# Loads of x in slots 10 to 16, the first convolution of the next image at the head of slot 10, and a gather without its tie to TensorE, in a kernel of grouped convolution and deformable bottleneck

## The reference

```python
x = x + _L0_conv_ref(_gn(x), W, b)           # 3x3, 8 groups; its result reshaped (B,G,gout,L)->(B,G,L,gout)->(B,512,32,32)
x = x + _L1_conv_ref(_gn(x), ...)            # the deformable bottleneck
# _L1_conv_ref:
out = relu(bn1(conv1x1(x, conv1_w)))         # 512 -> 128 channels
offset = conv3x3(out, off_w)                 # 18 offsets for each pixel
# deformable 3x3: for each tap and pixel a bilinear sample of out at a place that offset gives
val = v00*wy0*wx0 + v01*wy0*wx1 + v10*wy1*wx0 + v11*wy1*wx1
out = bn2(einsum('bckhw,ock->bohw', val, dconv_w))
out = relu(bn3(conv1x1(out, conv2_w)))       # 128 -> 512 channels
```

## Time and profile before

| what | value |
|---|---|
| median of 3 runs | 1756.08 us (1753.88 to 1757.5) |
| profiled execution | 1756.92 us, span 1755.1 us |
| PE busy | 1559.1 us (89%) |
| DVE busy | 1421.0 us (81%) |
| ACT busy | 955.4 us (54%) |
| POOL busy | 1183.5 us (67%) |
| gathers (q0), share of the DMA engines' time | 56.6%, 302.06 MB |
| SP's DMAs (q1) | 26.0%, 142.58 MB |

### The profile page before, as it was taken

One profiled execution on the slowest core, in us unless ns is written; L12 is line 12 of the kernel. 1 busy time (PEld: TensorE's weight loads), 2 busy tenths in 40 slices (PEclk: granted clock), 3 DMA queues, 4 the chain that ended last, 5 costly groups with the idle time before them and its releaser, 6 DMA issues.

```text
span 1755.1 us, 30014 instructions
## 1 busy us (share of the span) xinstructions
PE 1559.1 (89%) x9504; PEld 764.1 (44%) x9504; DVE 1421.0 (81%) x3577; ACT 955.4 (54%) x1411; POOL 1183.5 (67%) x1160
## 2 busy tenths in 40 slices
PE   4898899899998989999888998989899998988555
PEld 2454444445444544444344444545444443534221
DVE  6558798898989888797978979898897979887664
ACT  7665565565655646555655655556565555533222
POOL 0037777777777776776766767677677767777773
PEclk9998999999999999999999999999999999999766
DMA  9258879899897979889787988979798897978774
GB/s 245 54 175 238 273 221 293 244 283 297 260 309 232 324 223 286 266 262 303 234 290 219 288 279 250 315 228 325 218 299 271 261 300 226 284 232 271 213 248 140
DMA packets 161417, 446.63 MB, mean 254 GB/s; under 512 B 26598, under 2 KB 27238, under 8 KB 161254
## 3 DMA queue, kind: packets, MB, share of 16 engines
q0 software_dynamic: 92160, 302.06, 56.6%
q1 hardware_dynamic: 69094, 142.58, 26.0%
HBM read 373.23 MB, written 71.30 MB: 253 GB/s over the span
## 4 chain that ended last, share of the span: by engine, by line
PE 33%; issue 18%; DVE 17%; POOL 15%; DMA 13%; ACT 3%; POOLq 0%; DVEq 0%; SPq 0%; ACTq 0%
POOL sb_rows L376 15%; PE bank L834 12%; DMA sb_rows<-table,sb_ridx 10%; PE bank L809 5%; PE bank L903 5%; DVE sb_rows L613 5%; DVE sb_val L621 5%; PE bank L819 4%; PE bank L800 3%; DVE sb_split L653 3%; DMA table<-sb_table_sb 2%; PE bank L850 1%; DVE sb_raw L670 1%; PE bank L912 1%; PE bank L924 1%
## 5 line engine op out<-in xcount | busy, mean ns | idle before, releaser
L376 POOL DMA_INDIRECT sb_rows<-table,sb_ridx x1152 | 1179.7, 1024 | 527.2 <-issue 437.6
L613 DVE SCALAR_TENSOR_TENSOR sb_rows<-sb_rows,sb_frac 128x256 f32<-128x256 f32 x1152 | 505.3, 480 | 192.2 <-DMA sb_rows<-table,sb_ridx 186.4
L834 PE MATMUL bank<-sb_split,sb_wg 128*64 128x512 f16 x4608 | 572.5, 395 | 14.5 <-ACT sb_h_sb L481 8.1
L834 PEld LDWEIGHTS bank<-sb_split,sb_wg 128*64 128x64 f16 x4608 | 253.4, 111 | 314.3 <-issue 132.8
L621 DVE SCALAR_TENSOR_TENSOR sb_val<-sb_rows,sb_frac 128x128 f32<-128x128 f32 x1152 | 329.0, 347 | 15.3
L809 PE MATMUL bank<-sb_valT,sb_wd 128*128 128x512 f32 x576 | 329.6, 656 | 0.0
L800 PE MATMUL bank<-sb_eye_sb,sb_val 128*128 128x128 f32 x1152 | 195.7, 294 | 108.5 <-DVE sb_val L621 106.2
L404 ACT ACTIVATE sb_valT<-bank 128x512 f32<-128x512 f32 x288 | 173.7, 603 | 149.7 <-PE bank L800 149.5
L800 PEld LDWEIGHTS bank<-sb_eye_sb,sb_val 128*128 128x128 f32 x1152 | 126.0, 144 | 282.8 <-DVE sb_val L621 190.9
L426 ACT ACTIVATE sb_conv_sb<-bank,sb_bias 128x512 f32<-128x512 f32 x128 | 147.8, 1155 | 156.0 <-PE bank L834 150.8
L415 ACT ACTIVATE sb_res<-bank,sb_bn_t,sb_bn_s 128x512 f32<-128x512 f32 x128 | 99.3, 776 | 188.7 <-PE bank L819 187.7
(11 more groups left out here) (76 smaller groups left out, 1050.9 us busy)
## 6 DMA issues: line engine op xcount, KB each, us to landing
table<-sb_table_sb SPq DMA_DIRECT2D x144, 256.0 KB, 5.2
sb_xc<-x SPq DMA_DIRECT2D x64, 512.0 KB, 6.8
sb_xl<-x SPq DMA_DIRECT2D x128, 256.0 KB, 6.5
out<-sb_xl SPq DMA_DIRECT2D x128, 256.0 KB, 4.6
sb_rows<-table,sb_ridx POOLq DMA_INDIRECT x1152, 5.1
sb_rows<-w_group SPq DMA_DIRECT2D x8, 288.0 KB, 10.0
sb_wd<-w_def SPq DMA_DIRECT2D x1, 576.0 KB
sb_w<-w_in SPq DMA_DIRECT2D x1, 512.0 KB
```

The source lines that it names most:

```text
L376: pool.indirect_dma_start(out=rows[:, (c % RING) * PER + i, :], out_offset=None, in_=tables[u % 2], in_offset=bass.IndirectOffsetOnAxis(ap ...
L613: op = nc.vector.scalar_tensor_tensor(r[:, 0:2 * CH], r[:, 2 * CH:4 * CH], frac[:, parity, half * PER + i, k, 0:1], r[:, 0:2 * CH], ALU.mu ...
L834: op = nc.tensor.matmul(pair_ps[half][64 * e:64 * e + 64, :], wg[:, 2 * q + e, k, part * GIN:(part + 1) * GIN], plane(split1[:, 2 * q + e, ...
```

## The change

Three edits. Piece 0 of `new` goes from after the shuffle in slot 11 to the head of slot 10, and `NEXT_CONV` becomes 10. All four loads of x go into one step, in slots 10, 12, 14 and 16, so that none is left among the table's stores. POOL's wait for `valT_done` ahead of the third gather goes, with the semaphore increment behind it.

```diff
-        CONV_FIRST = {3: 7, 4: 8, 5: 9, 6: 10, 7: 11, 8: 13, 9: 14, 12: 1, 13: 3}
-        CONV_THEN = {2: 6, 7: 12, 9: 15, 11: 0, 12: 2, 16: 4, 17: 5}
-        NEXT_CONV = 11
+        CONV_FIRST = {3: 7, 4: 8, 5: 9, 6: 10, 7: 11, 8: 13, 9: 14, 10: 0, 12: 1, 13: 3}
+        CONV_THEN = {2: 6, 7: 12, 9: 15, 12: 2, 16: 4, 17: 5}
+        NEXT_CONV = 10
...
-        LOAD_X, LOAD_X_LATE = {14: 0, 17: 1}, {1: 2, 2: 3}
+        LOAD_X = {10: 0, 12: 1, 14: 2, 16: 3}
...
                     if a1 and new + 1 < IMAGES and s in LOAD_X:
                         load_x(new + 1, LOAD_X[s])
-                    if a1 and a2 and s in LOAD_X_LATE:
-                        load_x(new, LOAD_X_LATE[s])
...
                     pool.wait_ge(val_done, count(CHUNKS, t, c - RING + 1))
                     pool.sem_inc(pool_passed, 1)
                     for i in range(PER):
-                        if i == 2:
-                            pool.wait_ge(valT_done, count(CHUNKS, t, c - 2))
-                            pool.sem_inc(pool_passed, 1)
                         pool.indirect_dma_start(
```

## The result

The changed kernel takes 1745.66 us (median of 8 runs, 1735.2 to 1752.92), the kernel before 1757.89 us (8 runs, 1753.42 to 1762.69). The ratio is 0.9927 with an interval of 0.9898 to 0.9956, so it is faster by 0.7%, about 12 us. The forecast was 1718 us, 2.2% faster, with a range of 1690 to 1760 us: the direction was right, the size three times too large. The profiled execution took 1739.8 us, span 1738.0.

A forecast was written before the change was run, and what follows sets the result against it. PE, DVE and POOL were all near the period, so the once-per-image chain between them was taken as the bound. Terms of -24 + 5 - 9.5 - 8 - 2 = -38.5 us took 1756.9 to 1718.4 us, range 1690 to 1760.

The forecast's parts named there:

- The chain around the image: Image 9's loop: first gather 7.6, DVE to chunk 11's end 69.2, chunk 14 0.9, gathers 20.2, pause 3.5; sum 101.4 us.
- The last store comes 2.4 us earlier: Table stores in slots 2 and 3, freed of x loads: 1.36 + (6.1 - 5.1) us, -24 us over ten images.
- First failed step: POOL at chunk 14: starts 0.9 us after DVE's chunk 11, sixteen gathers following in 20.2 us, each gather taking 0.95 us.
- Second failed step: DVE's wait for PE at the second statistics: 0.95 us saved per image, -9.5 us over ten; bounds +2.1 and -2.3 per image.
- Piece 0: PE at slot 10's head: fills pauses, gains up to 5.8 us per image; -9.5 us counted, plus -2 before image 1.
- The tie: POOL's 44.8 us of waits for PE, mostly at chunks 8, 11, 12: ring wait replaces most, -8 us left.
- the three terms: Whole kernel: x loads -24 + 5 us, piece at slot 10 -9.5 - 2 us, POOL's wait for PE -8 us.
- Before the first gather: Image 1's piece on PE leaves ahead of image 0's second statistics, where DVE waits 4.11 us: -2 us, bounds 0 and -4.1.
- (a): Rival, chance 0.17: the early x load delays gathers DVE waits for, up to 3.9 us per image; 1768 us.
- (b): Rival, chance 0.14: the table stores' landing isn't due to x, so the pause at the image's head stays; 1747 us.
- (c): Rival, chance 0.09: everything falls to POOL's own rate, each period near 95.6 us; 1688 us.

The follow-up runs named there:

- the memsets: Two-column memsets ahead of each of DVE's four differences: added to the changed kernel 1721.11 us, ratio 0.9795; added to the kernel before 1744.1 us, ratio 0.9938.

## Why the prediction was wrong, point by point

- **The chain around the image was read rightly.** POOL's first gather to DVE's chunk 11 to POOL's chunk 14 and the table's landing is still the loop in image 9: 1020.3 to 1096.8, 0.8, 20.6 and 0.7 us.
- **"The last store comes 2.4 us earlier": right, and too small.** The stores of image 10's table issued from 1107 to 1113 land in 5.1 us, where it was 6.1, ACT's waits for stores of the table fell from 29.0 to 7.5 us in all, and the ten images lost 34 us of pause at their heads where 24 were forecast.
- **What came of it.** The loop of images 4 to 13 in the two profiled executions, mean us:

| part | before | changed |
|---|---|---|
| first gather to the end of chunk 11 | 76.9 | 76.9 |
| to chunk 14's first gather | 1.0 | 2.4 |
| to the end of the last gather | 20.5 | 20.5 |
| pause before the next image | 3.8 | 0.7 |
| period | 102.1 | 100.5 |

  The forecast was 3.5 us less per image: 2.4 by the table, 1.1 by the other terms. The pause gave 3.1. Two steps took the rest.
- **First failed step: that chunk 14 starts 0.9 us behind chunk 11 in every image, with every gather taken at 0.95 us.** In images 4, 6 and 10 it starts 5.0 us behind, in image 7 4.0 us, for the stuck gather ahead of it; that is the 1.4 us in the mean. Images 3 and 14 lose 4 us each in the same way. The sum had no row for a gather instruction that holds POOL, though the trace of before had it: two such of 5.1 and 6.2 us in images 0 and 1, and one of 1.99 us in nearly every later image. Breaking the run takes 24.6 us off the changed kernel and 12 off the kernel before; the difference, 12 us with an uncertainty of 8, is what the stuck gathers cost the change.
- **Second failed step: that of PE's gain the chain takes 0.95 us in each of ten images, -9.5 us.** The 0.95 us was image 9's. The kernel before has only five such waits in all (us in total, times, longest), the longest the one before the first gather, so that 3.5 us are left for the periods:

```profile
DVE sb_gs L687 <- PE bank L890: 7.6, 5, 4.1
```

  The first part of the loop didn't get shorter. DVE's stretch from chunk 0's fourth gather to the end of chunk 11 did a little, from 69.2 to 68.2 us in image 9 (ten images: 69.3 to 68.6; I had called the forecast failed if it stayed at 69), but what it gained the way to it lost. It isn't that the waits stayed: DVE's waits for chunk 0 fell from 1.45 to 0.13 us per image, for chunk 2 from 1.5 to 1.0, and image 9 reads chunk 0 (1027.47) without any:

```profile
1027.47 1.66 DVE L608 SCALAR_TENSOR_TENSOR sb_rows<-sb_rows,sb_frac 128x256 f32<-128x256 f32 x4
...
1038.35 0.49 DVE L608 SCALAR_TENSOR_TENSOR sb_rows<-sb_rows,sb_frac 128x256 f32<-128x256 f32 x1 [0.82 <-DMA sb_rows<-table,sb_ridx]
...
1076.57 0.69 DVE L623 TENSOR_TENSOR sb_xl<-sb_res,sb_xl 128x512 f32<-128x512 f32 x1 [1.42 <-ACT sb_res L410]
...
1088.22 0.69 DVE L623 TENSOR_TENSOR sb_xl<-sb_res,sb_xl 128x512 f32<-128x512 f32 x1 [0.83 <-ACT sb_res L410]
```

  So the pause's gain was passed on. But POOL now starts an image while DVE is still at work on the one before: DVE comes to chunk 0's fourth gather 8.4 us behind the first gather in the mean, not 7.6. And in image 9 the 0.95 us behind the second statistics went, but 1.42 + 0.83 = 2.25 us for ACT's relu came where those two waits had been 1.3.
- **Piece 0: the size came out, the mechanism isn't shown.** With the memsets in it gave 10 us (uncertainty 7) for 11.5, but the waits that it was to remove were only 3.5 us besides the one before the first gather. Without them it measured as no change, with five stuck gathers in images 2 to 13. That the numbers agree may be luck.
- **The tie: right that the ring takes its place.** Waits of 1.0 to 2.3 us at chunk 12 and 2.7 at chunk 14 replaced it. Its removal measured 5 us with and without the memsets, for the 8 forecast.
- **Luck.** That the changed kernel with the memsets measures 1721 us, 3 us from the forecast, is no support for it: the three terms were together some 13 us too large, and the memsets give the kernel before 12 us of their own. How the 13 us are shared among the three terms stays open.
- **Before the first gather: right in sign**, 3.6 us for 2 (bounds 0 and 4.1).
- **Rivals.** (a) and (b) didn't happen: the gathers beside the new load land about 1 us later, but DVE has no added waits for them, and the head's pause went. (c) was not reached: PE is at 94.7 of 98.6 us in image 9.

## What to carry to other kernels

When an edit shifts engines against each other, look at the longest instance of each repeated instruction, not its mean: a gather of 6 us among 0.95 us ones, however rare, tells of a place where the schedule can fall in. Ahead of a run of long DVE instructions with two inputs in SBUF try one very short instruction if POOL issues gathers meanwhile; here one memset of two columns per image was worth more (31 us by the ratios) than the three edits together (12 us). Before a wait is priced from one image, look in the view of waits how often it occurs. And a pause that looks like pure loss may go along with something useful, as DVE's pause for ACT's relu does here.

## What the runs showed of the hardware that was not expected

- POOL's gather instruction of 0.95 us was held until 0.82 us after the end of a DVE instruction (1.99 us beside one difference), and beside an unbroken run of the residual add and four differences, these some 1.3 us apart, until 0.82 us after the last, 6.62 us in all.
- A short instruction in that run (0.06 us with no input, 0.15 us with two inputs in SBUF) lets the gather in at its place.
- Where DVE had paused just ahead of the run (60 of 135 runs), no gather was held beyond 2.14 us; all 65 runs with a gather held to the end are among the 75 without the pause. The start of the gather doesn't tell: at 2.17 us behind the first difference it was held to the end nine times and by one difference five times, at 0.35 us once each, at -0.26 to -0.23 us once to the end and eight times by the residual add alone, and each time the pause parts them.
- Why a pause of DVE before the run, or one short instruction, lets a gather in at a later seam is open. So is why ten runs without the pause have no stuck gather; in six of them the gather began 0.12 us ahead of the first difference and was held by the add alone. Whether a difference with one input in SBUF would hold a gather wasn't tried, nor a break in DVE's other runs.
